# Operands of TensorE on multiples of 128 bytes, router logits with x stationary, and the last normalizing on ScalarE, in a four-layer kernel

## The reference

```
# linear attention, 16 heads of 32
q, k = relu(q), relu(k)
vk  = einsum('bhen,bhdn->bhed', v_pad, k)
out = einsum('bhed,bhdn->bhen', vk, q)
out = out[:, :, :-1] / (out[:, :, -1:] + EPS)
x   = layernorm(x + out @ w_proj.T + b_proj)

# experts; x is (4, 512 tokens, 512)
logits = einsum('btd,de->bte', x, Wr)              # 8 per token
inhibition = sigmoid(logits / temperature)
in_zone = (inhibition >= GOLDEN_LOWER) & (inhibition <= GOLDEN_UPPER)
distance = abs(inhibition - GOLDEN_CENTER)
w  = exp(-distance / 0.1) * in_zone
fb = exp(-distance / 0.3)                          # kept for the top 2, normalized
w  = where(w.sum() < 1e-8, fb_w, w);  w = w / w.sum()
mid = silu(x @ Wg[e] + low rank) * (x @ Wu[e] + low rank)
out = mid @ Wd[e] + low rank
x   = layernorm(x + sum_e w[e] * out[e])
```

## Time and profile before

| | |
|---|---|
| time, median of 3 runs | 2444.58 us (2443.91 to 2445.42) |
| profiled execution: its own time | 2445.11 us |
| its span | 2443.4 us |
| mean clock granted to TensorE | 0.974 of full speed |
| PE busy | 2319.7 us (95%) |
| PEld busy | 1869.5 us (77%) |
| DVE busy | 1596.3 us (65%) |
| ACT busy | 845.6 us (35%) |
| POOL busy | 715.8 us (29%) |
| DMA | 155.37 MB |

### The profile page before, as it was taken

One profiled execution on the slowest core, in us unless ns is written; L12 is line 12 of the kernel. 1 busy time (PEld: TensorE's weight loads), 2 busy tenths in 40 slices (PEclk: granted clock), 3 DMA queues, 4 the chain that ended last, 5 costly groups with the idle time before them and its releaser, 6 DMA issues.

```text
span 2443.4 us, 30703 instructions
## 1 busy us (share of the span) xinstructions
PE 2319.7 (95%) x10684; PEld 1869.5 (77%) x10684; DVE 1596.3 (65%) x2371; ACT 845.6 (35%) x1363; POOL 715.8 (29%) x515
## 2 busy tenths in 40 slices
PE   8997999999979999997999799999999899999997
PEld 7786788888857888885887678777778788888885
DVE  5556667777747956675354766667677886666665
ACT  5445222222214322222132244334354444444441
POOL 0002334444421222221121333233233543333331
PEclk9998999999989999998999999999999999999999
DMA  5644222222223001001000211212101121111100
GB/s 202 221 147 153 59 69 69 69 69 70 72 81 135 18 18 35 1 1 40 1 1 1 72 58 52 78 78 78 52 26 52 52 87 52 52 52 52 52 35 35
DMA packets 91012, 155.37 MB, mean 64 GB/s; under 512 B 6288, under 2 KB 55440, under 8 KB 84256
## 3 DMA queue, kind: packets, MB, share of 16 engines
q1 hardware_dynamic: 90912, 154.07, 18.7%
HBM read 114.20 MB, written 39.85 MB: 63 GB/s over the span
## 4 chain that ended last, share of the span: by engine, by line
PE 47%; DVE 5%; issue 1%; ACT 1%; POOL 0%; POOLq 0%; DVEq 0%; ACTq 0%
PE attn_pvk L1483 5%; PE attn_pvk L1482 5%; PE attn_pvk L1484 4%; PE attn_pq L1482 2%; PE attn_pq L1483 2%; PE attn_pq L1484 2%; PE attn_po L1483 2%; PE attn_po L1482 2%; PE attn_pv L1482 2%; PE attn_po L1484 2%; PE attn_pv L1483 2%; PE attn_pv L1484 2%; PE attn_pv L86 1%; PE attn_pv L88 1%; PE attn_pv L87 1%
## 5 line engine op out<-in xcount | busy, mean ns | idle before, releaser
L2452 DVE TENSOR_TENSOR moe_a_lo<-moe_up_raw,moe_a_hi 128x512 fp32r<-128x512 f32 x192 | 181.6, 962 | 160.8 <-ACT moe_a_hi L1929 160.7
L1408 DVE SCALAR_TENSOR_TENSOR acc<-ffn_pd,ffn_wts,acc 128x512 f32<-128x512 f32 x256 | 178.2, 749 | 90.4 <-PE ffn_pd L88 90.0
L1822 POOL TENSOR_TENSOR moe_h_lo<-moe_c_t,moe_h_hi 128x512 fp32r<-128x512 f32 x96 | 128.6, 1340 | 363.1 <-ACT moe_h_hi L1929 363.1
L1482 PE MATMUL attn_pvk<-moe_b_hi,moe_a_hi 128*128 128x512 f32 x512 | 204.0, 398 | 12.8 <-ACT moe_c_last L2052 5.2
L1483 PE MATMUL attn_pvk<-moe_b_lo,moe_a_hi 128*128 128x512 f32 x512 | 205.5, 401 | 0.0
L1484 PE MATMUL attn_pvk<-moe_b_hi,moe_a_lo 128*128 128x512 f32 x512 | 200.6, 392 | 0.0
L1929 ACT ACTIVATE moe_c_t<-attn_pvk 128x512 f32<-128x512 f32 x192 | 113.8, 598 | 198.3 <-PE attn_pvk L1484 198.3
L1102 POOL TENSOR_TENSOR ffn_h_lo<-ffn_h_f,ffn_h_hi 128x512 fp32r<-128x512 f32 x64 | 89.8, 1404 | 281.9 <-ACT ffn_h_hi L1165 281.9
L1981 ACT ACTIVATE moe_c_t<-moe_c_t 128x512 f32<-128x512 f32 x96 | 60.4, 629 | 246.1 <-DVE moe_c_t L2524 246.1
L1929 ACT ACTIVATE moe_a_hi<-moe_up_raw 128x512 fp32r<-128x512 f32 x192 | 115.8, 623 | 56.4 <-POOL moe_up_raw L1793 56.4
L1482 PEld LDWEIGHTS attn_pvk<-moe_b_hi,moe_a_hi 128*128 128x128 f32 x512 | 96.8, 189 | 40.1 <-issue 10.9
(11 more groups left out here) (439 smaller groups left out, 6426.4 us busy)
## 6 DMA issues: line engine op xcount, KB each, us to landing
moe_up_raw<-in_e_up SPq DMA_DIRECT2D x28, 1024.0 KB, 5.8
moe_dn_raw<-in_e_dn SPq DMA_DIRECT2D x28, 512.0 KB, 3.7
xh<-in_out_hi SPq DMA_DIRECT2D x32, 256.0 KB, 2.6
zs<-in_out_z SPq DMA_DIRECT2D x32, 256.0 KB, 3.2
xl<-in_out_lo SPq DMA_DIRECT2D x32, 256.0 KB, 3.4
ssd_z_raw<-zs SPq DMA_DIRECT2D x16, 512.0 KB, 3.9
in_w_raw<-in_in_w SPq DMA_DIRECT2D x4, 1024.0 KB, 6.9
x<-xh SPq DMA_DIRECT2D x8, 512.0 KB, 4.1
```

The source lines that it names most:

```text
L1408: stt(out=acc[:, ch], in0=pd[:, c], scalar=w, in1=acc[:, ch], op0=ALU.mult, op1=ALU.add).then_inc(s_acc, 1)
L1482: pe.matmul(out, lh, rh, start=first, stop=False, skip_group_check=True)
L1822: tt(h_lo[:, m, tok], src, raw(h_hi[:, m, tok]), ALU.subtract).then_inc(s_hlo, 1)
L2452: tt_(a_lo[q][:], src, raw(a_hi[q][:]), ALU.subtract).then_inc(s_alo, 1)
```

## The change

Four parts.

1. `Map.sb` places every tile of at least 2048 bytes per partition on a multiple of 128 bytes. By the addresses of the built program all large tiles of experts and attention then start on one. SSD's tiles stay where they are.
2. The logits are made by one function for both pairs: `xr` is the stationary operand (128 by 128), `rw_raw` (8 columns) the moving one, and tokens come out on partitions. That is 32 fp32 matmuls of 8 columns for a pair: in chunk 13 ahead of k's product, and in slot 11 at its first step. The split parts of the weights, the ACT copies and the transposes go, and slot 11 takes one bank of the ring where it took three.
3. The router's parts move: part 0 and its ACT function into chunk 13, part 1 behind chunk 13, part 2 behind chunk 14, part 3 into chunk 15. ACT takes its functions behind the copy of `qT`.
4. In the tail, `norm_out` of chunks 11 to 15 moves from DVE to ACT (`Identity` with `bias=shift`, `scale=rstd`), POOL makes `shift` = -mean * rstd with two more operations, and the order of DVE, PE and POOL is rewritten: each `divide` stands ahead of the `norm_in` of the chunk before, and slot 0's first three up products go one step earlier.

```diff
     def sb(self, name, shape, dt=F32):
-        offset = self.pos
-        self.pos += (4 * math.prod(shape[1:]) + 31) // 32 * 32
+        size = 4 * math.prod(shape[1:])
+        line = 128 if size >= 2048 else 32
+        offset = (self.pos + line - 1) // line * line
+        self.pos = offset + size
...
             def deviation(m):
                 inverse_deviation(nc, pool, amv[:], arstd[:], const[:], s_amv, s_aeps, s_arstd, m + 1)
+                if m >= TAIL - 1:
+                    nc.gpsimd.tensor_tensor(shift[:], amv[:, 0:1], const[:, 2:3], ALU.mult).then_inc(s_shift, 1)
...
+                    nc.gpsimd.tensor_tensor(shift[:], shift[:], arstd[:], ALU.mult).then_inc(s_shift, 1)
...
+            def norm_out(m):
+
+                act.wait_ge(s_shift, 2 * (m - TAIL + 1) + 2)
+                nc.scalar.activation(acc[:, m], rr[:], ACT.Identity, bias=shift[:], scale=arstd[:]).then_inc(s_ln, 1)
...
-            def logits(bank, b):
-                for kt in range(KT):
-                    ins = pe.matmul(bank[0:NE], rw_raw[:, kt], xr[:, kt, bass.ts(b, SEQ)], start=kt == 0, stop=kt == KT - 1)
-                return ins
-
-            def logits_of_parts(bank):
-                for kt in range(KT):
-                    q, i = kt // 2, kt % 2
-                    pe.matmul(bank[0:2 * NE], rw[:, kt], b_hi[q][:, i], start=kt == 0, stop=False)
-                    ins = pe.matmul(bank[0:NE], rw[:, kt, 0:NE], b_lo[q][:, i], start=False, stop=kt == KT - 1)
-                return ins
-
-            def turn_logits(bank, log_t, parts=False):
+            def logits(bank):
                 for c in range(PC):
-                    w = 2 * NE if parts and c < CPB else NE
-                    ins = pe.transpose(bank[:, c * 2 * NE:c * 2 * NE + w], log_t[c // CPB][0:w, bass.ts(c % CPB, P)],
-                                       ident[0:w, 0:w])
+                    for kt in range(KT):
+                        ins = pe.matmul(bank[:, c * NE:(c + 1) * NE], xr[:, kt, bass.ts(c, P)], rw_raw[:, kt],
+                                        start=kt == 0, stop=kt == KT - 1)
                 return ins
...
-                if n == PLAIN_AT:
-                    pe.wait_ge(s_lgc, 1)
-                    pe.wait_ge(s_xr, PC)
-                    logits(pt[:], 1).then_inc(s_lg, 1)
+                if n == TOKENS_AT:
+                    pe.wait_ge(s_small, 32)
+                    logits(pt[:]).then_inc(s_wts, 1)
...
             for c in range(CPB):
-                m = NCH - CPB + c
+                m = TAIL + c
+                if c < len(FIRST):
+                    up(0, *FIRST[c])
                 pe.wait_ge(s_olo, m + 1)
                 turn_out(m)
                 if c < CPB - 1:
                     attend(m + 1)
-                if c:
-                    ring.enter(0)
-                    up(0, *FIRST[c - 1])
                 pe.wait_ge(s_pa, m if c else m + 1)
                 project(m, (pv, pq)[c % 2])
...
+                    dve.wait_ge(s_lgt, 1)
+                    router(0, 0)
+                if n == TOKENS_AT + 2:
+                    router(0, 3)
                 dve.wait_ge(s_v, n + 1)
...
-            for c in range(CPB):
-                m = NCH - CPB + c
-                divide(m)
-                if c:
-                    norm_out(m - 2)
-                low_out(m)
-                norm_in(m - 1, (pv, pq)[(c - 1) % 2] if c else pv)
-                if c == 0:
-                    router(0, 3)
-                if c < 3:
-                    x_low(0, (4, 2, 3)[c])
-            norm_out(NCH - 2)
+            divide(TAIL)
+            x_low(0, 4)
+            low_out(TAIL)
+            divide(TAIL + 1)
+            norm_in(TAIL - 1, pv)
+            low_out(TAIL + 1)
+            divide(TAIL + 2)
+            norm_in(TAIL, pv)
+            x_low(0, 2)
```

More of the change, by code:

```diff
@@ L1591, in attn_experts @@
         first_cmp = [scratch[:, i * DM:(i + 1) * DM].rearrange("p (c i j) -> p c i j", c=PC, i=NE) for i in (0, 1)]
-        first_log = [scratch[0:2 * NE, i * DM:(i + 1) * DM] for i in (2, 3)]
         xrf = xr[:].rearrange("p k n -> p (k n)")
@@ L1658, in ring_of @@
             known = (0, 0, 8, 16, 24, 32, 46, 60, 74, 88, 96, 112)
-            return known[n] if isinstance(n, int) and n < 12 else 8 * n + 27
+            return known[n] if isinstance(n, int) and n < 12 else 8 * n + 25
         def slots(eng, slot):
@@ L1810, in x_sums @@
                 if part == 2:
-                    pool.wait_ge(s_lg, 2)
+                    pool.wait_ge(s_wts, 1)
                     tt(b12, b22, b12, ALU.subtract).then_inc(s_bsum, 1)
+                if part == 3:
                     pool.wait_ge(s_blo, 7 * pair + 2)
@@ L1848, in slot @@
                     x_sums(1, 2)
+                    x_sums(1, 3)
             pool.wait_ge(s_bias, 16)
@@ L1859, in _ @@
                     weight_sums(0, 0, 0, 2)
-                if n == PLAIN_AT:
+                if n == TOKENS_AT - 1:
                     x_sums(0, 0)
-            deviation(NCH - CPB - 1)
             x_sums(0, 1)
-            deviation(NCH - CPB)
+            deviation(TAIL - 1)
             x_sums(0, 2)
-            for m in range(NCH - CPB + 1, NCH):
+            deviation(TAIL)
+            x_sums(0, 3)
+            for m in range(TAIL + 1, NCH):
                 deviation(m)
@@ L1891, in ahead_x @@
                                      ACT.Copy).then_inc(s_xr, 1)
-            def logits_copy(b):
-                rows = 2 * NE if b == 0 else NE
-                act.wait_ge(s_lg, b + 1)
-                nc.scalar.activation(first_log[b][0:rows], pt[0:rows], ACT.Copy).then_inc(s_lgc, 1)
             def chunk(n):
@@ L2025, in slot @@
                 take(n, 1, 2, s_u2, 1, 2)
+                if at(n, 0):
+                    norm_out(NCH - 1)
                 if at(n, SLOTS - 1):
@@ L2066, in _ @@
                     up_high(0, 0, 0, 1)
-                    act.wait_ge(s_small, 32)
-                    copy(rw[:, :, 0:NE], rw_raw[:]).then_inc(s_rwhi, 1)
                 if n == 9:
@@ L2710, in _ @@
                     up_low(0, 0, 5)
-                if n == 13:
-                    dve.wait_ge(s_lgt, 1)
-                    router(0, 0)
-                if n == 14:
+                if n == TOKENS_AT:
                     router(0, 1)
-                if n == 15:
+                if n == TOKENS_AT + 1:
                     router(0, 2)
-            for c in range(CPB):
-                m = NCH - CPB + c
-                divide(m)
-                if c:
-                    norm_out(m - 2)
-                low_out(m)
-                norm_in(m - 1, (pv, pq)[(c - 1) % 2] if c else pv)
-                if c == 0:
-                    router(0, 3)
-                if c < 3:
-                    x_low(0, (4, 2, 3)[c])
-            norm_out(NCH - 2)
+            divide(TAIL)
[7 more added lines that the diff above has]
+            x_low(0, 2)
+            low_out(TAIL + 2)
+            divide(TAIL + 3)
+            norm_in(TAIL + 1, pq)
+            x_low(0, 3)
+            low_out(TAIL + 3)
+            norm_in(TAIL + 2, pv)
             x_low(0, 5)
-            norm_in(NCH - 1, (pv, pq)[(CPB - 1) % 2])
             x_low(0, 6)
-            norm_out(NCH - 1)
+            norm_in(TAIL + 3, pq)
             for n in range(SLOTS + 2):
```

94 lines of the change are left out of this document (38 added, 56 removed).

## The result

The changed kernel took 2434.42 us (median of 5 runs, 2432.84 to 2437.21), beside 2445.42 for the kernel before in the same session: ratio 0.9958, 95% interval 0.9944 to 0.9973. Measured once more later (beside experiment 6), it had a ratio of 0.9978 (0.9969 to 0.9987). The forecast was 2430.

The account below looks back on a forecast made before the run. TensorE, busy 95% of the span, was taken as the bound. The terms -14.9 - 0.6 + 0.5 + 9.2 - 1.6 - 7.0 = -14.4 took the median from 2444.6 to 2430 us, with a range of 2419.5 to 2440.

Parts of the forecast that it names:

- alignment, experts and projections: Expert slots and attention projections: aligned operands speed up matmuls, -14.9 us in slots and -0.6 in projections.
- logits in chunks 12 and 13, PE and clock: Chunks 12 and 13: new passes for old work cost +1.25 us, the lump's low clock 4.6 more.
- logits in slot 11, PE and clock: Slot 11: new passes for old work give -0.75 us, the lump's low clock costs 4.6.
- waits for ACT in chunks 14 and 15: Chunks 14 and 15: q's relu no longer queued behind router functions, 1.1 and 0.5 us, -1.6 in all.
- chunk 15 and tail to the last projection's end: Chunk 15 to the last projection: its end moves by -3.6 us, against +2.4 for a low clock in chunk 15.
- slot 0 to the start of slot 1: Slot 0: PE's wait of 3.69 us for ACT shrinks to 0.5, -3.2, and the low clock behind gives -2.6.
- the rival at 2446: Expert slots and projections: the offset is not the cause, 15.5 us of gain are missing, no difference; chance 0.08.
- Clock: Logits in chunk 13 and slot 11: the clock falls in each lump of 64 passes, 4.6 us each, +9.2.
- The rival at 2421: Logits lumps in chunk 13 and slot 11: no fall of the clock, so 9.2 us less; chance 0.13.
- Loads of `xr` do not overlap: Logits lumps: each pass takes 0.192 us, 10.4 us more twice, 2451, slower than before; chance 0.03.
- Chunk 15: Chunk 15: DVE's copy of v comes 3.6 us later, PE idles some 4 us, the low clock costs 2.4.
- Norms on ACT: Tail: normalizing on ACT delays `norm_out` some 0.3 us, nobody waits, so zero; without that cover 1.5 us.

Follow-up runs that it names:

- experiment 6: The changed kernel with the tail's norms back on DVE and DVE's old order there; ratio 0.9987 to the kernel before.
- align_only: The kernel before with only the new placement of tiles, and the tile flag put on top of `sel` for room; ratio 0.9943 to the kernel before.
- after_32: The changed kernel with placement back on multiples of 32 bytes, the other three parts kept; ratio 1.0017 to the kernel before.
- dn_at_32: The changed kernel with the down products' moving operands `dn_hi` and `dn_lo` 32 bytes off; 1318.7 us from attention's start to the end.
- spread: The changed kernel with the same 64 logits passes in groups between other products in chunk 13 and slot 11; ratio 0.9947 to the kernel before.
- rank_later: The changed kernel with part 3 of the router behind the masking of the products in chunk 15; ratio 0.9951 to the kernel before.
- experiment 5: The changed kernel with the tail's normalizing back on DVE, POOL's shift operations gone, the new order kept; ratio 0.9982 to the kernel before.

## Why the prediction was right, and where it was off

The time lay inside the range, the sign and the two large mechanisms were right, and the gain came out short of the 14.4 us forecast: 7.6 by the traces, 10.3 and 5.4 by the two ratios. Term by term, from attention's start:

| term | forecast | measured |
|---|---|---|
| alignment, experts and projections | -15.5 | -15.7 (align_only) |
| logits in chunks 12 and 13, PE and clock | +5.9 | +5.7 |
| logits in slot 11, PE and clock | +3.9 | +3.7 (41.96 for 38.24) |
| waits for ACT in chunks 14 and 15 | -1.6 | -1.4 |
| chunk 15 and tail to the last projection's end | -1.2 | -0.7 |
| slot 0 to the start of slot 1 | -5.8 | +0.6 (-0.7 and -0.8 in after_32 and dn_at_32, same order) |
| sum | -14.4 | -7.8 (7.6 in the traces) |

*Alignment.* Right in cause and size, shown by doing it alone. The offset costs 0.56 us in a slot of 30.48, and the rival at 2446, that it is not the cause, is out. The Trainium skill (SBUF — State Buffer, section Operand start alignment) calls its rule a matter of legality, not speed, and says that its runs timed nothing. The prediction read "worth nothing" into it, which the page doesn't state.

*Clock.* Right in cause and near in size: 4.6 us a lump were forecast as its price. In slot 11 the spread version is 4.6 shorter, pass time included, and the trace shows the clock falling while PE was busy for 9.11 of 9.11 us. The rival at 2421 is out. The account of the Trainium skill (TensorE: Matmul & The Clock Gate, section HAM oscillation — how this bites in real kernels), which has the clock drop in idle gaps between bursts, is not all there is: in this lump there was no gap.

*Loads of `xr` do not overlap.* Out: eight passes take 0.95 us in the timeline of spread, so less than 0.12 each at full clock, though the load of each has a duration of 0.19 on record as in the earlier trace rows. (The rival's formula, 128 s - 2.2, gives 12.5 us for s = 0.115, not the 11.95 that stands beside it; that changes nothing here.)

*Chunk 15.* Right: DVE's copy of v came 3.9 us late (3.6 forecast), PE waited 4.24 us for it, the clock fell in the projection behind it. rank_later shows that the place of part 3 is the cause.

*Slot 0.* This is the step that failed: "In slot 0 PE waits 3.69 for ACT, whose queue was held up by the late high parts of x; these come earlier relative to PE, and I leave 0.5 of the wait: -3.2", and with it -2.6 for the low clock behind. From the end of the last projection to slot 1 it was 23.9 us before and is 24.5 now. The high parts of x did not hold ACT's queue before. ACT had finished them and stood idle for DVE's first sum of slot 0:

```profile
1400.44 0.63 ACT L1981 ACTIVATE moe_c_t<-moe_c_t 128x512 f32<-128x512 f32 x1 [7.72 <-DVE moe_c_t L2524]
```

DVE reaches that sum only behind the last residual sum and its statistics. It was at 266.5 us from attention's start before and is at 268.5 now. From the residual sum to it 7.8 us became 3.5, but the residual sum itself starts 6.2 us later (265.0 for 258.8), since the whole tail starts later and each `norm_in` waits for the one before.

*Norms on ACT.* The prediction put these at zero, since nobody would wait for `norm_out` until the next residual sum. ACT itself waited for it: 3.01 us for POOL's `shift`, with slot 0's copies behind it in ACT's queue, and PE 2.8 us for the copy. Taking this hold away (experiment 5) gained nothing, since DVE's first sum then came later. Neither the norms' engine (5) nor DVE's order (6) took the two waits away; each moved time between them. What would, such as the last `norm_in` behind slot 0's first sum, wasn't tried, and so it stays open which link of this chain is the tightest.

## What to carry to other kernels

Put every large operand of TensorE on a multiple of 128 bytes, both the moving and the stationary one: here that alone gave 15.7 us, twice what the whole change did. Don't put many short products in one lump on TensorE, even with no wait in it: spread between long ones the same 64 passes were 4.0 and 4.6 us cheaper at two places. Where executions differ in phases that the change doesn't touch, compare traces from a mark behind those phases. Then check stretches behind the mark whose code is the same, too: here they still differed by up to 1.7 us.
